# Autocorrelation attention and a gated expert layer on one core: q folded twice, x mirrored on load, and x plus the attention output formed in the dense layer

## The reference

```python
# x, ctx: (8, 512, 2048) float32
x = x + tanh(g_xattn) * autocorrelation(layernorm(x), ctx, ctx)
x = x + tanh(g_ffn) * ffn(layernorm(x))

def autocorrelation(Q, K, V):          # every channel by itself, along the 512 positions
    corr = ifft(fft(Q) * conj(fft(K))).real
    w, idx = top_k(corr, 12); w = softmax(w)
    out[t] = sum_i w[i] * V[min(idx[i] + t, 511)]

def ffn(x):                            # per row of 2048
    base = x @ W_base.T + b_base
    adapted = softmax(x @ W_gate.T) - sigmoid(x @ W_thr + b_thr) * 0.125
    w = normalised(where(adapted >= 0, adapted, 0))        # 8 experts of rank 16
    return base + 2 * sum_e w[e] * B[e] @ (A[e] @ x)
```

## Time and profile before

| | |
|---|---|
| median of 3 runs | 3030.46 us (3029.5 to 3032.73) |
| profiled execution | 3031.29 us |
| its span, first to last instruction | 3029.5 us |
| PE busy | 2921.9 us (96%) |
| DVE busy | 1606.0 us (53%) |
| POOL busy | 1454.0 us (48%) |
| ACT busy | 1012.6 us (33%) |
| DMA | 324.49 MB, mean 107 GB/s |
| TensorE clock granted | 0.990 of full on average |

### The profile page before, as it was taken

How to read it: one execution, slowest core, us unless ns; L and a number is a source line. 1 busy time by engine, 2 the same in 40 slices (tenths; PEclk the granted TensorE clock), 3 DMA queues, 4 the chain that set the end, 5 groups by cost and what they waited for, 6 DMA issues and landing times.

```text
span 3029.5 us, 37059 instructions
## 1 busy us (share of the span) xinstructions
PE 2921.9 (96%) x13184; PEld 1466.0 (48%) x13184; DVE 1606.0 (53%) x2738; ACT 1012.6 (33%) x1672; POOL 1454.0 (48%) x577
## 2 busy tenths in 40 slices
PE   4999999999999999997799999999999999999999
PEld 2445554555545554553644444444444444444444
DVE  3899989999999999998722121121211112111111
ACT  4555556555555545441511121111211112111110
POOL 4788888889888888884031211212112121221210
PEclk8999999999999999999899999999999999999999
DMA  8455544555455554423634132331323313233230
GB/s 201 124 123 126 139 110 118 127 132 125 115 122 125 135 117 102 101 73 111 237 98 111 56 111 75 91 111 55 111 72 94 106 60 111 69 97 99 68 97 28
DMA packets 260355, 324.49 MB, mean 107 GB/s; under 512 B 162911, under 2 KB 163487, under 8 KB 245541
## 3 DMA queue, kind: packets, MB, share of 16 engines
q1 hardware_dynamic: 259922, 323.38, 40.1%
q10 hardware_dynamic: 348, 0.18, 0.0%
HBM read 223.76 MB, written 67.21 MB: 96 GB/s over the span
## 4 chain that ended last, share of the span: by engine, by line
PE 84%; DVE 5%; POOL 3%; issue 2%; DMA 2%; ACT 1%; SPq 1%; ACTq 0%; DVEq 0%; POOLq 0%
PE bank L1097 43%; PE bank L488 7%; PE bank L422 7%; PE bank L454 6%; PE bank L472 5%; PE bank L460 3%; POOL spec_o L869 3%; DVE rows_mem L1256 2%; PE bank L1086 1%; PE bank L1087 1%; PE bank L1088 1%; ACT wt L548 1%; PE bank L435 1%; PE bank L405 1%; PE bank L411 1%
## 5 line engine op out<-in xcount | busy, mean ns | idle before, releaser
L1281 POOL TENSOR_TENSOR rows_mem<-norm,rows_mem 128x2048 f16<-128x2048 f32 x31 | 126.1, 4068 | 1220.7 <-ACT rows_mem L1156 1220.7
L1097 PE MATMUL bank<-w_hi,rows_mem 128*128 128x512 f16 x2048 | 489.3, 379 | 3.8 <-DVE rows_mem L1256 3.8
L1097 PE MATMUL bank<-w_hi,xres_mem 128*128 128x512 f16 x2048 | 489.0, 379 | 3.5 <-DVE rows_mem L1256 3.5
L869 POOL TENSOR_TENSOR spec_o<-spec_o,term 128x1024 f32<-128x1024 f32 x190 | 443.3, 2362 | 40.6 <-DVE term L686 40.6
L1249 DVE TENSOR_TENSOR hwt_lo<-bank,hwt_hi 128x128 f16<-128x128 f32 x32 | 9.3, 292 | 790.4 <-ACT hwt_hi L1175 790.4
L1097 PEld LDWEIGHTS bank<-w_hi,rows_mem 128*128 128x128 f16 x2048 | 200.2, 98 | 251.6 <-DVE rows_mem L1256 13.6
L1097 PEld LDWEIGHTS bank<-w_hi,xres_mem 128*128 128x128 f16 x2048 | 200.2, 98 | 250.6 <-DVE rows_mem L1256 12.7
L488 PE MATMUL bank<-spec_o,table 128*128 128x512 f32 x512 | 249.1, 617 | 19.9 <-POOL spec_o L869 15.8
L1097 PE MATMUL bank<-w_lo,xres_mem 128*128 128x512 f16 x1024 | 262.8, 379 | 0.0
L1097 PE MATMUL bank<-w_lo,rows_mem 128*128 128x512 f16 x1024 | 262.8, 379 | 0.0
L422 PE MATMUL bank<-rows_mem,table 128*128 128x512 f32 x512 | 227.7, 598 | 18.0 <-POOL rows_mem L849 15.7
(11 more groups left out here) (182 smaller groups left out, 4876.3 us busy)
## 6 DMA issues: line engine op xcount, KB each, us to landing
rows_mem<-in_x_dram SPq DMA_DIRECT2D x32, 1024.0 KB, 13.0
norm<-x_scratch SPq DMA_DIRECT2D x32, 1024.0 KB, 5.5
rows_mem<-x_scratch SPq DMA_DIRECT2D x32, 1024.0 KB, 7.0
out_dram<-rows_mem SPq DMA_DIRECT2D x32, 1024.0 KB, 4.4
norm<-in_x_dram SPq DMA_DIRECT2D x28, 1024.0 KB, 10.8
rows_mem<-in_ctx_dram SPq DMA_DIRECT2D x256, 64.0 KB
rows_mem<-in_ctx_dram SPq DMA_DIRECT2D x64, 256.0 KB
xres_mem<-in_x_dram SPq DMA_DIRECT2D x256, 64.0 KB
```

Source lines behind the costliest of these rows:

```text
L869: pool.tensor_tensor(to, to, buffer, sign).then_inc(term_added, 1)
L1097: mm = pe.matmul(dense[o][:, :], nt(par, part)[:, k, :], w[:, k, o * 512:(o + 1) * 512], start=(k == 0 and n == 0), stop=False)
L1281: pool.tensor_tensor(norm_lo, norm[:, :], norm_hi, ALU.subtract).then_inc(norm_lo_made, 1)
```

## The change

The spectra of q now use the symmetry that v's used already: the table is centred on the middle of 512 positions, x is loaded in mirrored order, `fold_q` folds twice (four operations instead of two), and `q_spectra` makes 4 products with `v_tab` instead of 8 with `q_tab`. The spectra of q(i+1) are made in step i, between the two output parts. The sums of q·k go from GpSimd to VectorE, which writes two of its products back into PSUM. `residual` is gone: ScalarE copies the gated output parts (cosine and sine) out of PSUM (`keep_out`), SP stores them in natural order, for positions ahead of the middle and behind it, and the dense layer forms x2 = x + cosine part ∓ sine part on GpSimd (`form`), from loads on ScalarE's queue. It keeps x2 in memory and `row` has one buffer; rounding of tile i+1 is one step later than before. In the prologue the first batch's moments are taken from natural rows, loaded on ScalarE's queue, and turned into mirrored order by two small matmuls; the first fold of q is VectorE's.

```diff
+    def load_mirrored(to, after, before, i, loaded):
         b, c = i // NCH, (i % NCH) * C
         sp.nop(nofuse=True)
...
+            sp.dma_start(to[16 * n:16 * n + 16, 0:2, :], after[b, 7 - n, :, :, ds(c, C)]).then_inc(loaded, 16)
         for h in range(2):
-            sp.dma_start(vt[:, 2 + h, :], v_before[b, :, :, h, ds(c, C)]).then_inc(v_loaded, 16)
+            sp.dma_start(to[:, 2 + h, :], before[b, :, :, h, ds(c, C)]).then_inc(loaded, 16)
...
     def load_x(i):
         if least(i) >= 1:
-            sp.wait_ge(q_folded, 2 * i)
...
+            sp.wait_ge(q_folded, 4 * (i - 1) + 2)
+        load_mirrored(xt, x_after, x_before, i, x_loaded)
...
+    def store(i):
+        sp.wait_ge(out_kept, 2 * (i + 1))
...
         for n in range(8):
...
+            sp.dma_start(parts[1][2 * b:2 * b + 2, :, 112 - 16 * n:128 - 16 * n, c:c + C].rearrange("h a p c -> p (h a) c"),
+                         kept[16 * n:16 * n + 16].rearrange("p h a c -> p (h a) c")).then_inc(parts_stored, 16)
         for h in range(2):
...
+            for a in range(2):
+                sp.dma_start(parts_ahead[2 * b + h, a, :, :, c:c + C], kept[:, h, a, :]).then_inc(parts_stored, 16)
...
-        sp.dma_start(xstat[:, :, :], x_t[b, :, :, ds(c, C)]).then_inc(xstat_loaded, 16)
+        load_mirrored(xstat, x_after, x_before, n, xstat_loaded)
...
     load_v(0)
-    sp.dma_start(table[:, :], tables[:, 0:I_AT]).then_inc(table_loaded, 16)
...
-    for n in range(NCH):
-        sp.dma_start(early[n], x_t[0, :, :, n * C:(n + 1) * C]).then_inc(early_loaded[n], 16)
...
-            load_v_last(0)
     load_x(0)
-    sp.dma_start(ident[:, :], tables[:, I_AT:I_AT + 128]).then_inc(ident_loaded, 16)
+    load_v_last(0)
+    sp.dma_start(table[:, P_AT:I_AT], tables[:, P_AT:I_AT]).then_inc(table_loaded, 16)
...
     load_v(1)
     load_v_last(1)
+    load_x(1)
+    sp.dma_start(table16[:, :], tables16).then_inc(table16_loaded, 16)
     load_stats(NCH)
-    load_x(1)
     load_stats(NCH + 1)
...
     def step(i, par, phase):
-        if i < STEPS:
-            load_res(i, par)
...
+        if i == STEPS - 2:
+            first_tile()
         if i == STEPS - 1:
-            first_norm()
+            sp.wait_ge(formed, 2)
+            sp.dma_start(x2_rows[0], norm[:, :]).then_inc(x2_kept, 16)
             for m in range(4):
                 early_weights(m)
         if i >= 1:
-            store(i - 1, 1 - par)
...
+        sp.wait_ge(parts_stored, 192 * NCH)
+        sp.dma_start(norm[:, :], x_rows[0]).then_inc(first_loaded, 16)
+        sp.wait_ge(q_folded, 4 * STEPS)
+        for n in range(2):
+            sp.dma_start(rows_mem[:, n, :], parts[0][0, n]).then_inc(first_loaded, 16)
...
     def q_spectra(i, four):
-        pe.wait_ge(q_folded, 2 * (i + 1))
+        pe.wait_ge(q_folded, 4 * (i + 1))
         for half in range(2):
             pe.wait_ge(v_copied, 4 * i + 3 + half)
             for row in range(2):
-                for j in range(2):
-                    mm = pe.matmul(pair(four, half)[:, row, :], q_tab[:, 2 * half + row, j, :],
-                                   qf[:, 2 * row + j, :], start=(j == 0), stop=(j == 1))
+                mm = pe.matmul(pair(four, half)[:, row, :], v_tab[:, 2 * half + row, :],
+                               q_sym[:, 2 * half + row, :], start=True, stop=True)
             mm.then_inc(q_made, 1)
...
-                pe.wait_ge(sine_added, 4 * (c - 1) + 2 * (y + 1))
+                pe.wait_ge(out_kept, 2 * (c - 1) + y + 1)
...
-        pe.wait_ge(prod_made, 2 * (i + 1))
+        pe.wait_ge(q_used, 2 * (i + 1))
...
-    pe.wait_ge(table_loaded, 16)
+    pe.wait_ge(v_tab_loaded, 16)
     pe.wait_ge(last_tab_made, 1)
     v_spectra(0, 0, X(0))
...
+    pe.wait_ge(order_made, 2)
+    pe.wait_ge(ln1_step, 6)
+    for n in range(2):
+        mm = pe.matmul(bank[7][:, 4 * n:4 * n + 4], order[:, n, :], ln1_rows[:, :, 1 - n::2], start=True, stop=True)
+    mm.then_inc(ln1_turned, 1)
+    q_spectra(0, X(0))
+    pe.wait_ge(table_loaded, 16)
...
     def step(i, par, phase):
         mine, other = X(par), X(1 - par)
-        if most(i) < STEPS:
-            q_spectra(i, mine)
         if least(i) >= 1:
...
+        if most(i) + 1 < STEPS:
+            q_spectra(i + 1, other)
+        if least(i) >= 1:
             out_tiles(i - 1, (phase - 1) % NCH, mine, 0)
...
+    def keep_out(c, four, h):
+        if h == 1 and least(c) >= 1:
+            act.wait_ge(parts_stored, 192 * c)
+        act.wait_ge(out_made, 2 * c + 2 - h)
+        act.activation(kept[:, h, :, :], pair(four, 1 - h), ACT.Copy, scale=gates[:, 0:1]).then_inc(out_kept, 1)
...
+    act.dma_start(table[:, 0:P_AT], tables[:, 0:P_AT]).then_inc(v_tab_loaded, 16)
+    act.dma_start(ident[:, :], tables[:, I_AT:I_AT + 128]).then_inc(ident_loaded, 16)
...
+    for t in range(TT):
+        act.dma_start(early[t], x_rows[t]).then_inc(early_loaded[t], 16)
...
+    for n, view in enumerate((blocks[:, ::-1, :], blocks[:, :, ::-1])):
+        act.activation(order[:, n, :].rearrange("k (n p) -> k n p", p=16), view, ACT.Copy).then_inc(order_made, 1)
...
     copy_v(0, 0, X(0), False)
-    copy_v(0, 0, X(0), True)
     deviation(0)
     normalise(0)
+    copy_v(0, 0, X(0), True)
...
+        if least(i) >= 1:
+            keep_out(i - 1, mine, 1)
         if most(i) < STEPS:
             scale_w(i)
+        if least(i) >= 1:
+            keep_out(i - 1, mine, 0)
...
-        dve.tensor_tensor(prod_a[:, 0:2, :], real, k[:, 1:3, :], ALU.mult)
-        dve.tensor_tensor(prod_b[:, 2:4, :], real, k[:, 3:5, :], ALU.mult).then_inc(q_used, 1)
+        dve.tensor_tensor(prod_a[:, 0:2, :], real, k[:, 1:3, :], ALU.mult).then_inc(qk_made, 1)
+        dve.tensor_tensor(prod_b[:, 2:4, :], real, k[:, 3:5, :], ALU.mult).then_inc(qk_made, 1)
         dve.wait_ge(q_made, 2 * i + 2)
-        dve.tensor_tensor(prod_b[:, 0:2, :], imag, k[:, 3:5, :], ALU.mult)
-        dve.tensor_tensor(prod_a[:, 2:4, :], imag, k[:, 0:3:2, :], ALU.mult).then_inc(q_used, 1)
+        dve.wait_ge(qk_made, 4 * i + 2)
+        dve.tensor_tensor(real, imag, k[:, 3:5, :], ALU.mult).then_inc(qk_made, 1)
+        dve.tensor_tensor(imag, imag, k[:, 0:3:2, :], ALU.mult).then_inc(qk_made, 1)
+        dve.wait_ge(qk_made, 4 * i + 3)
+        dve.tensor_tensor(prod_a[:, 0:2, :], real, prod_a[:, 0:2, :], ALU.add).then_inc(q_used, 1)
+        dve.wait_ge(qk_made, 4 * i + 4)
+        dve.tensor_tensor(prod_a[:, 2:4, :], imag, prod_b[:, 2:4, :], ALU.subtract).then_inc(q_used, 1)
...
-            dve.scalar_tensor_tensor(out=xres[:, par, h, :, :], in0=pair(four, 1 - h)[:, 0:1, :].to_broadcast([128, 2, C]),
-                                     scalar=gates[:, 0:1], in1=xres[:, par, h, :, :], op0=ALU.mult, op1=ALU.add)\
-               .then_inc(cos_added, 1)
-        for n, h in enumerate((1, 0)):
-            dve.wait_ge(cos_added, 2 * c + n + 1)
-            for at, gate in enumerate((gates[:, 0:1], gate_neg[:, :])):
-                dve.scalar_tensor_tensor(out=xres[:, par, h, at, :], in0=pair(four, 1 - h)[:, 1, :], scalar=gate,
-                                         in1=xres[:, par, h, at, :], op0=ALU.mult, op1=ALU.add).then_inc(sine_added, 1)
...
+        if most(i) == STEPS:
+            moments(dve, 0)
         if least(i) >= 1:
             w_low(i - 1, other)
+        if most(i) == STEPS:
+            scale_rows(dve, 0)
+        if least(i) >= 1:
             w_times_v(i - 1, 1 - par, mine, other, 0)
         if least(i) >= 1:
             w_times_v(i - 1, 1 - par, mine, other, 1)
...
-    for n in range(NCH):
...
+    for t in range(TT):
+        early_stats(t)
...
-    scales(0)
-    dve.wait_ge(gates_ready, 2)
+    newton(dve, ln1_step, 0, ln1_sqrt, 1, var, std, tmp, mv[:, :, 0], ln1_rows[:, 0], ln1_rows[:, 1], 1.0)
+    dve.wait_ge(ln1_turned, 1)
+    turned = bank[7][:, 0:8].rearrange("p (s w h) -> p s w h", s=2, w=2)
+    dve.tensor_copy(ln1_scale[:, :].rearrange("p (s h) -> p s h", s=2), turned[:, :, 0, :])
+    dve.tensor_copy(ln1_bias[:, :].rearrange("p (s h) -> p s h", s=2), turned[:, :, 1, :]).then_inc(ln1_ready, 1)
+    fold_q(dve, 0)
...
+def fold_q(eng, i):
+    if least(i) >= 1:
+        eng.wait_ge(q_made, 2 * i)
+    eng.wait_ge(x_normed, 4 * (i + 1))
+    eng.tensor_tensor(qf[:, 0:2, :], xt[:, 0:4:2, :], xt[:, 1:4:2, :], ALU.add).then_inc(q_folded, 1)
+    eng.tensor_tensor(qf[:, 2:4, :], xt[:, 0:4:2, :], xt[:, 1:4:2, :], ALU.subtract).then_inc(q_folded, 1)
+    eng.wait_ge(q_folded, 4 * i + 2)
+    eng.tensor_tensor(q_sym[:, 0:2, :], qf[:, 0:4:2, :], qf[:, 1:4:2, :], ALU.add).then_inc(q_folded, 1)
+    eng.tensor_tensor(q_sym[:, 2:4, :], qf[:, 0:4:2, :], qf[:, 1:4:2, :], ALU.subtract).then_inc(q_folded, 1)
...
+    def first_tile():
+        pool.wait_ge(first_loaded, 48)
+        pool.tensor_tensor(norm[:, :], norm[:, :], rows_mem[:, 0, :], ALU.add).then_inc(formed, 1)
+        pool.wait_ge(formed, 1)
+        pool.tensor_tensor(norm[:, :], norm[:, :], rows_mem[:, 1, :], ALU.subtract).then_inc(formed, 1)
...
```

(92 more changed lines are left out.)

201 lines of the change are left out of this document (81 added, 120 removed).

## The result

The changed kernel takes 3027.16 us (median of 20 runs, 3020.13 to 3028.93), the kernel before 3030.04 (20 runs, 3028.11 to 3032.80): ratio over all runs 0.9986, 95% interval 0.9980 to 0.9992 (the medians alone give 0.9990). The forecast was 2990 with 2950 to 3026. Case 4's time (3030) was measured, but not by its mechanism: in the steady steps fold q waits for nothing.

A forecast was written before the change was run, and what follows sets the result against it. TensorE bounds both stages, with GpSimd nearly as full in attention and setting the new step. Steps −40.2, prologue +8, end of attention −2.7 and −6, dense 0 sum to −40.9, giving 2990 us, range 2950 to 3026.

The forecast's parts named there:

- Case 4: Attention steps: fold q's x waits for the mirrored load, GpSimd idles the 1.8 gained, 3030 us; chance 0.06.
- The step in GpSimd's terms: Attention step: 16 GpSimd operations at 2.33, 0.3 for own waits and 3.10 before fold v make 40.7 us.
- Rival 1: Attention steps: selection isn't held or slips between GpSimd's operations, TensorE's 39.2 sets the step, 2960 us; chance 0.17.
- selection and GpSimd's work never overlap: Attention step: VectorE's selection, with two SBUF inputs, stands still while GpSimd works, giving GpSimd's 3.10 us wait before fold v.
- loses `residual`, 2.9 less: VectorE in an attention step: loses 5.3 us of residual, takes two q·k sums of 1.2 each, 2.9 less.
- New scales, 2.6 every fourth step: Every fourth attention step GpSimd waits 5.72 instead of 3.10 for new layer-norm scales: 2.6 us more, seven times.
- Product into PSUM 1.2: VectorE's two products written into PSUM in an attention step: 1.2 us each, bounds 1.2 and twice that.
- Prologue +8: Before step 1: longer mirrored loads on SP's queue delay v(2), landing at 90; +8 us, bounds +2 and +14.
- End of attention: After the last steps: −2.7 us at the turning that waited for the residual, −6 from an earlier last store.
- Dense stage 0: Dense layer: TensorE's work stays 47.0 us a tile, cost 0, with 7 us to spare for the two loads.
- rival 3: Dense layer becomes a chain: loads land in 10.8, 3.6 us over the room a tile, 3102 us; chance 0.13.
- 2 (late x): Attention steps: normalised x comes late for fold q, 0.8 us a step in the middle, 3015 us; chance 0.14.

The follow-up runs named there:

- one_sum_small: Changed kernel with VectorE's loop border moved and first statistics chunk loaded before x(1), plus one GpSimd w·v sum cut to 16 elements a partition: 2946.79 us.
- no_yield: Changed kernel with VectorE's loop border moved and first statistics chunk loaded before x(1), without GpSimd's wait for the selection ahead of fold v: 3140.02 us.
- vector_unrolled: Changed kernel with VectorE's steps 2 to 25 written out, other engines keeping their loops: 3007.63 us, 0.9929 of the kernel before.
- before_unrolled: Kernel before the change with VectorE's steps 2 to 25 written out, nothing else changed: 3029.40 us, ratio 0.9995.
- turned_loop: Changed kernel with VectorE's loop border moved between the low parts of w and the products of w and v: 3007.57 us, ratio 0.9928.
- b_later: Changed kernel with VectorE's loop border moved, first statistics chunk loaded before x(1), and B issued behind step 2's store: 2992.67 us, 0.9881 of the kernel before.
- best: Changed kernel with VectorE's loop written out, first statistics chunk loaded before x(1), and B issued behind step 2's store: 2990.60 us, 0.9871 of the kernel before.

## Why the prediction was wrong

- **The step in GpSimd's terms: right.** 40.3 for the 40.7 forecast, with the waits of 1.28 and 0.49 gone and one of 2.81 left; one sum less took 1.7 off the step (one_sum_small). Rival 1 (TensorE's 39.2) is not what ran, but 39.7 is the step once GpSimd is out of the way. The reason given for the 2.81, that selection and GpSimd's work never overlap, is too strong: in no_yield they overlap, one operation for one, at 2.8 each.
- **VectorE "loses `residual`, 2.9 less": the step that failed.** It was counted as busy time saved. It also covered VectorE's loop branch. The saving itself shortened no step as far as the waits show, GpSimd being the bound (no run tests it alone); the cover was worth 3.0 in five steps, 15 us (vector_unrolled, before_unrolled, turned_loop). The prediction asked what hides an edit costed at nothing, and not what the removed work itself was hiding. Half of the price, 2.6 of the 5.4 in a turn, is a second effect, TensorE's clock after the longer stop. The other 1.7 of the 16.7 us lost in the steps are a balance: steps 1 and 2 took 47.4 and 44.4, 7.8 over the sum, and all the rest together 6 under it.
- **New scales, 2.6 every fourth step: right**, 2.1 to 2.2 where no branch falls (42.4 against 40.3).
- **Product into PSUM 1.2: right**, 1.23 for L682.
- **Prologue +8: mis-sized**, +19.8 and +14.2 in two executions, the bound given being +14. The chain down SP's queue was followed to the right end (v(2)), but landed there at 104.7 instead of 90, late in its own terms: x(1) was issued to 54.3 instead of 47, because the half of VectorE's first fold that it waits for, placed at 42, ended at 49.3; the first chunk, issued at 54.8 to 60.9, landed at 67.8 instead of 56; the second landed at 84.2 instead of 69.5. And ScalarE's order was left out: the chunks hold `copy_odd`, and so the first selection, which ended at 103.6. Of the length of step 1 part is B's issues (b_later).
- **End of attention: the three gains about right, the longer store left out.** From the last fold v on, the forecast has −6.6 for the steps' last work, −2.7 for the turning and −6 for the start of the last store. Measured from the traces: GpSimd's last full sum ends 5.5 sooner, the last output tile another 2.6, the store starts another 6.0 (1.2 behind the last tile instead of 7.2). But the store is twelve issues now and takes 9.1 us instead of 6.2, and W_base's rows stand behind it on SP's queue: 3.0 of the 4.5 lost. The prediction names the twelve issues and gives them no price (timelines of SP; before, the store began at 1448.99 and W_base's rows as shown first):

```profile
1455.16 28.83 SPq L999 DMA_DIRECT2D rows_mem<-in_L_ffn_W_base_dram  x12
```

```profile
1437.89 4.47 SPq L313 DMA_DIRECT2D parts_behind<-parts_mem  x8
1442.40 4.57 SPq L317 DMA_DIRECT2D parts_ahead<-parts_mem  x4
1447.02 29.00 SPq L1021 DMA_DIRECT2D rows_mem<-in_L_ffn_W_base_dram  x12
```

- **Dense stage 0: right from tile 2 on, +5.3 in tiles 0 and 1.** 47.47 a tile, as before; the 47.0 that the prediction read as a tile is half of the stretch that it had chosen, not a period. The two loads land in 5.7 and 4.9, and the last thing ahead of `hw_hi` in ScalarE's queue is issued 4.5 us before `hw_hi` is due (timeline of ScalarE; for 7 forecast):

```profile
2233.40 0.35 ACTq L1197 DMA_DIRECT2D norm<-in_x_dram  x1
2243.81 0.34 ACTq L1206 DMA_DIRECT2D rows_mem<-parts_behind  x1
2253.33 0.36 ACTq L1211 DMA_DIRECT2D x_scratch<-norm  x1
2253.90 0.34 ACTq L1201 DMA_DIRECT2D rows_mem<-parts_ahead  x1
2258.42 0.28 ACT L1186 ACTIVATE hwt_hi<-bank 128x128 f16<-128x128 f32 x1 [29.50 <-PE bank L1113]
```

  In tile 0 x of tile 1 is loaded only from 1492.8 on, behind the weights, and x2 formed from 1504.0 on, and TensorE waits 3.1 for its transposes; in tile 1 `hw_hi` stands behind `keep_x2` as in rival 3, once (TensorE's timeline):

```profile
1544.04 0.22 PE L1094 MATMUL bank<-parts_mem,rows_mem 128*128 128x137 f16 x1 [3.08 <-DMA rows_mem<-rows_mem]
...
1596.49 0.38 PE L1120 MATMUL bank<-corr_mem,hwt_hi 128*128 128x512 f16 x1 [1.82 <-DVE hwt_lo L1296]
```

- **Rivals.** 2 (late x), 3 (the chain beyond tile 1) and 4 (fold q's load in the steady steps) did not happen. With the branch gone, the chunk moved and B later (`best`), the kernel takes the 2990 that was forecast, but that agreement is partly luck, since the parts don't agree: prologue +4.2 for +8, 29 steps −40.1 for −33.6, end of attention −13.5 for −15.3, from there on +9.0 for 0.

## What to carry to other kernels

When work is taken from an engine that is not the bound, ask what that work covered: a loop branch or a wait. Where an issue list grows, price what stands behind it on the same queue. Put an engine's loop border where operations are queued ahead of the branch, or write that one engine's loop out. Where one engine waits in its order for a load that is not urgent (statistics of the next batch), look at what stands behind it, on its own queue and on the one that issues the load.

## What the runs showed of the hardware

VectorE's branch back to the start of its loop is followed by 2.8 to 3.05 us without an instruction issued, 3.6 to 3.7 with the moved border, with two 8 KB transfers of instructions near it; where the loop was left, the next instruction came after 0.11. GpSimd's and ScalarE's turns took 0.24 to 0.28, with some 140 and 250 records of instructions a turn against VectorE's 360; TensorE's took 0.3 at most with 1220, so the count alone doesn't explain it (what does wasn't tried). A stop of 3.9 us cost TensorE a further 2.6 through its clock (16 matmuls at 6.19 instead of 3.61); stops of 2.6 us in the written-out kernel were followed by the lower clock as well (5.30). While GpSimd works back to back, VectorE's operations with two SBUF inputs go one for each of GpSimd's: 2.8 us each on 512 elements a partition, with GpSimd's slowed from 2.37 to 2.8, and 2.2 each on 4 elements, with GpSimd's unchanged.
